# First batch's normalisations inside the second scan on ScalarE instead of VectorE, with softmax sums and gate remainders in PSUM

## What is computed

```python
# layer 0, mixer: normalise, project, convolve, then the selective scan
h = exp(dt_t * A) * h + (dt_t * x_t) * B_t ;  y_t = h @ C_t      # 256 steps, 256 x 16 states
y = (y + xc * D) * silu(z) ;  out = clamp(layernorm(clamp(y @ out_proj_w.T)))
x = x + out                                                        # skip
# layer 0, experts
t = layernorm(x) ;  xn = layernorm(t) * ln_g + ln_b
probs = softmax(xn @ gate_w) ;  combine = the two largest probs, 0 elsewhere
out = sum_e combine[:, e] * (gelu(xn @ w1[e] + b1[e]) @ w2[e] + b2[e])
t = x + layernorm(x) + out
# layer 1: x + decay scan over a row of channels, layernorm, 16 experts, top 2, no bias
```

## Time and profile before

| | us |
|---|---|
| median of 3 runs | 215.6 |
| lowest, highest | 214.52, 215.91 |
| profiled execution, its own time | 212.92 |
| its span in the trace | 211.0 |
| TensorE busy with matmuls | 180.6 |
| VectorE busy | 135.5 |
| ScalarE busy | 120.1 |
| GpSimd busy | 104.4 |

### The profile page before, as it was taken

One profiled execution on the slowest core, in us unless ns is written; L12 is line 12 of the kernel. 1 busy time (PEld: TensorE's weight loads), 2 busy tenths in 40 slices (PEclk: granted clock), 3 DMA queues, 4 the chain that ended last, 5 costly groups with the idle time before them and its releaser, 6 DMA issues. The chain is left out here.

```text
span 211.0 us, 3706 instructions
## 1 busy us (share of the span) xinstructions
PE 180.6 (86%) x1194; PEld 149.6 (71%) x1194; DVE 135.5 (64%) x317; ACT 120.1 (57%) x276; POOL 104.4 (49%) x136
## 2 busy tenths in 40 slices
PE   6789677995887387499999999699998999999993
PEld 5467454542353243267999989699997999999992
DVE  2764689999899999972373846563158573433433
ACT  2717995999850039143578646567564655455540
POOL 5410034579796955475575435444456244444500
PEclk9999999999999979999999999999999999999998
DMA  6950199995540000000000000000000000000000
GB/s 182 307 153 0 59 393 341 324 321 165 199 165 37 2 0 0 0 0 0 3 2 0 3 2 0 3 0 0 3 2 0 3 0 5 0 26 3 0 0 25
DMA packets 7233, 14.38 MB, mean 68 GB/s; under 512 B 512, under 2 KB 3112, under 8 KB 6960
## 3 DMA queue, kind: packets, MB, share of 16 engines
q1 hardware_dynamic: 7216, 14.17, 20.8%
HBM read 13.88 MB, written 0.29 MB: 67 GB/s over the span
## 5 line engine op out<-in xcount | busy, mean ns | idle before, releaser
L343 POOL TENSOR_TENSOR hc<-hs,cb 128x1024 f32<-128x1024 f32 x16 | 37.7, 2356 | 32.6 <-DVE hs L712 32.6
L836 DVE SCALAR_TENSOR_TENSOR acc<-dbx_ps,comb,acc 128x128 f32<-128x128 f32 x96 | 29.1, 344 | 36.6 <-PE dbx_ps L1106 35.6
L1081 PE MATMUL bc_ps<-x_hi,w_hi 128*128 128x256 f32 x128 | 41.8, 326 | 0.0
L563 ACT ACTIVATE hid<-bc_ps,par 128x256 f32<-128x256 f32 x64 | 26.8, 469 | 24.9 <-PE bc_ps L1083 24.8
L357 POOL TENSOR_TENSOR w_lo<-w1b,w_hi 128x256 fp32r<-128x256 f32 x32 | 23.5, 735 | 27.6 <-ACT w_hi L555 27.3
L712 DVE TENSOR_TENSOR_SCAN hs<-da,dbx_ps 128x1024 f32<-128x1024 f32 x16 | 36.5, 2278 | 0.1
L1083 PE MATMUL bc_ps<-x_hi,w_lo 128*128 128x256 f32 x128 | 36.2, 283 | 0.0
L1082 PE MATMUL bc_ps<-x_lo,w_hi 128*128 128x256 f32 x128 | 36.0, 281 | 0.0
L1106 PE MATMUL dbx_ps<-w2a,hid 128*128 128x128 f32 x256 | 34.1, 276 | 0.5 <-issue 0.3
L1106 PE MATMUL dbx_ps<-w2b,hid 128*128 128x128 f32 (+1 forms) x256 | 33.9, 276 | 0.5 <-DVE acc L836 0.5
L357 POOL TENSOR_TENSOR w_lo<-w1a,w_hi 128x256 fp32r<-128x256 f32 x32 | 23.1, 729 | 21.6 <-ACT w_hi L555 21.6
(11 more groups left out here) (164 smaller groups left out, 227.1 us busy)
## 6 DMA issues: line engine op xcount, KB each, us to landing
w1a<-w_in SPq DMA_DIRECT2D x2, 1024.0 KB, 9.0
cb<-c_rows SPq DMA_DIRECT2D x2, 1024.0 KB, 6.8
w1b<-w_in SPq DMA_DIRECT2D x2, 1024.0 KB, 13.7
cb<-c_rows SPq DMA_DIRECT2D x2, 768.0 KB, 5.2
cb<-taps_in SPq DMA_DIRECT2D x1, 512.0 KB, 5.2
cb<-c_rows SPq DMA_DIRECT2D x2, 256.0 KB, 3.8
par<-packed_in SPq DMA_DIRECT2D x1, 473.0 KB, 3.4
x_cm<-x_in SPq DMA_DIRECT2D x2, 128.0 KB, 2.2
```

The lines of the kernel that those rows point to most:

```text
L343: nc.gpsimd.tensor_tensor(hc[p][:], hs[p][:], cb[:, k].rearrange("p i (o t) -> p i o t", o=1).to_broadcast([128, PAIR, DC, T]), ALU.mult). ...
L563: ins = nc.scalar.activation(hid[p][:, c, :], h_ps[:, p, T * c:T * (c + 1)], ACT.Gelu, bias=par[:, bass.ds(u * UC + at, 1)])
L836: nc.vector.scalar_tensor_tensor(acc[k][:, t, :], o_ps[:, w // span % RING, 128 * t:128 * (t + 1)], comb[layer][b][:, t, bass.ds(u, 1)], a ...
L1081: nc.tensor.matmul(h_ps[:, p, T * c:T * (c + 1)], w1_hi[w][:, at], x_hi[b][:], start=True, stop=False)
```

## The change

Batch 0's normalisations of `skip_norm` and `inner_norm` are made by ScalarE as rstd * x + shift; GpSimd makes the new column `shift` = -mean * rstd after `root_3` and after `root_4`. `skip_scale` is a new step ahead of scan 2. ScalarE also scales `xg_tok` (`inner_scale`) and copies `combT` (`gates_tc`) for batch 0. VectorE keeps the clamp, the sums and the statistics, and all of batch 1. In every gating the remainder after the two largest (`left`) stands in PSUM instead of SBUF, and in `softmax_e` so does the reciprocal of the sum. In the diff `shifted` and the lines behind it are GpSimd's, `skip_scale` to the first `gates_tc` ScalarE's, and what follows from `skip_norm` VectorE's.

```diff
+        shift = sb("shift", [128, TT])
-        left = [[sb(f"left_{l}_{b}", [128, TT, EXPERTS[l] + 8]) for b in range(NB)] for l in range(2)]
+        m_zsum = m_ps[:, T + 32:T + 32 + TT]
+        m_left = [m_ps[:, T + 64:T + 64 + TT * (n + 8)].rearrange("p (t e) -> p t e", t=TT) for n in EXPERTS]
-        before_states = {1: ["gate_out", "out_proj"], 3: ["inner_norm", "root_5"], 4: ["logits"], 5: ["softmax_e"],
+        before_states = {1: ["gate_out", "out_proj"], 2: ["skip_scale"], 3: ["inner_norm", "root_5"], 4: ["logits"], 5: ["softmax_e"],
...
+            def shifted(k):
+
+                link(nc.gpsimd.tensor_tensor(shift[:], mv[0][:, :, 0], rstd[0][:], ALU.mult))
+                nc.gpsimd.tensor_scalar(shift[:], shift[:], -1.0, None, ALU.mult).then_inc(s["shift" + k], 1)
...
+                    if b == 0 and step in ("root_3", "root_4"):
+                        pool.wait_ge(s["rstd" + which], 1)
+                        shifted(which)
...
+            def skip_scale(layer, b):
+                act.wait_ge(s["shift3"], 1)
+                for t in range(TT):
+                    ins = nc.scalar.activation(m_norm[:, t, :], norm_a[b][:, t, :], ACT.Identity, scale=rstd[b][:, t:t + 1],
+                                               bias=shift[:, t:t + 1])
+                ins.then_inc(s["skip_scaled"], 1)
+
+            def inner_norm(layer, b):
+                if b:
+                    return
+                act.wait_ge(s["shift4"], 1)
+                for t in range(TT):
+                    ins = nc.scalar.activation(m_tok[:, t, :], t_tok[b][:, t, :], ACT.Identity, scale=rstd[b][:, t:t + 1],
+                                               bias=shift[:, t:t + 1])
+                ins.then_inc(s["inner_done"], 1)
+
+            def inner_scale(layer, b):
+                if layer or b:
+                    return
+                act.wait_ge(s["rstd5"], 1)
+                act.wait_ge(s["sum_done"], 1)
+                for t in range(TT):
+                    ins = nc.scalar.activation(xg_tok[b][:, t, :], m_tok[:, t, :], ACT.Identity, scale=rstd_b[b][:, t:t + 1])
+                ins.then_inc(s["xn_tok"], 1)
+
+            def gates_tc(layer, b):
+                if b:
+                    return
+                act.wait_ge(s["comb_ps"], b + 1)
+                nc.scalar.activation(combT[b][:], m_ps[0:EXPERTS[0], 0:T], ACT.Copy).then_inc(s["combT_ready"], 1)
...
             def skip_norm(layer, b):
                 dve.wait_ge(s["xtok_ready"], b + 1)
-                link(normalise(TT, m_norm, norm_a[b], mv[b], rstd[b], "rstd3", b))
+                if b:
+                    link(normalise(TT, m_norm, norm_a[b], mv[b], rstd[b], "rstd3", b))
+                else:
+                    dve.wait_ge(s["skip_scaled"], 1)
                 link(clamp(m_norm, m_norm))
...
             def inner_norm(layer, b):
-                link(normalise(TT, m_tok, t_tok[b], mv[b], rstd[b], "rstd4", b))
+                if b:
+                    link(normalise(TT, m_tok, t_tok[b], mv[b], rstd[b], "rstd4", b))
 
             def inner_scale(layer, b):
+                if (layer, b) == (0, 0):
+                    dve.wait_ge(s["inner_done"], 1)
+                    nc.vector.tensor_tensor(t_tok[b][:], t_tok[b][:], m_tok, ALU.add).then_inc(s["sum_done"], 1)
+                    return
...
-                link(nc.vector.reciprocal(zsum[b][:], zsum[b][:]))
+                link(nc.vector.reciprocal(m_zsum, zsum[b][:]))
                 link(nc.vector.tensor_tensor(prob[layer][b][:, :, 0:n], ex[:],
-                                             zsum[b][:].rearrange("p (t o) -> p t o", o=1).to_broadcast([128, TT, n]), ALU.mult))
+                                             m_zsum.rearrange("p (t o) -> p t o", o=1).to_broadcast([128, TT, n]), ALU.mult))
...
-                pr, rest_p = prob[layer][b], left[layer][b]
+                pr, rest_p = prob[layer][b], m_left[layer]
...
             def gates_tc(layer, b):
+                if b == 0:
+                    return
                 dve.wait_ge(s["comb_ps"], b + 1)
```

More of the change, by code:

```diff
@@ L85 @@
 b_ready dbx_done da_done h_done hc_done y_done
-yz_ready o_ps var3 rstd3 var4 rstd4 rstd5 xn_tok xn_ps x_full x_hi_ready xsplit logit_ps z_sub z_tanh comb_ready
+yz_ready o_ps var3 shift3 skip_scaled inner_done sum_done shift4 rstd3 var4 rstd4 rstd5 xn_tok xn_ps x_full x_hi_ready xsplit logit_ps z_sub z_tanh comb_ready
 comb_ps combT_ready b2_ps
@@ L528, in stage @@
                 high_part(0, u, u)
+            def skip_scale(layer, b):
[23 more added lines that the diff above has]
+                    return
+                act.wait_ge(s["comb_ps"], 1)
+                nc.scalar.activation(combT[b][:], m_ps[0:EXPERTS[0], 0:T], ACT.Copy).then_inc(s["combT_ready"], 1)
             def exp_logits(layer, b):
@@ L586, in _ @@
                     "bc_copy": bc_copy, "silu1": silu1, "stage": stage,
-                    "pair_in": pair_in, "exp_logits": exp_logits, "expert_in": expert_in,
+                    "pair_in": pair_in, "exp_logits": exp_logits, "skip_scale": skip_scale, "inner_norm": inner_norm, "inner_scale": inner_scale,
+                    "gates_tc": gates_tc, "expert_in": expert_in,
                     "softmax": softmax, "experts": experts}
```

## The result

The changed kernel takes 221.53 us (median of 4, 220.68 to 222.50) against 215.19 for the kernel before in the same comparison: ratio 1.0295, interval 1.023 to 1.036, 6.3 us more. Forecast were 3.3 more. Its four executions lie in two pairs (220.68 and 220.86, 222.19 and 222.50 us); the profiled one took 220.68 us, span 218.9.

A forecast was written before the change was run, and what follows sets the result against it. VectorE (97% busy) bounds the second scan; the start of TensorE's expert run at the first output matmul sets the end. Delay 0.97 inherited plus 2.56 new, less 0.23, gives +3.3 on 215.6: 218.9 us, range 217 to 221.

The forecast's parts named there:

- the queue's sum: Batch 1's scan to first output matmul: waits in ScalarE's ordered queue delay it 3.53 us; less 0.23 regained, +3.3 us.
- 94.96: Predicted time in us of TensorE's first output matmul in the changed kernel, instead of 91.43 before.
- VectorE's three waits: Signs in batch 1's scan: VectorE idle about 1.5 us before the t_tok sum, about 1.6 before scan 4, over 2 before scan 7.
- rival (d): ScalarE's switch to the Gelu table costs another 1.28 us beyond its load: 4.6 us in all, 220.2 us; chance 0.02.
- the term for TensorE's clock: At the first output matmul: the forecast sum added nothing for a lower TensorE clock behind the gap.
- rival (c): TensorE's clock halves for 3 us behind the gap before the first output: 1.5 us more, 4.8 in all, 220.4; chance 0.13.
- same pace of 1.6 us a unit: Sign of a right forecast: after the first output matmul, TensorE's expert work keeps 1.6 us a unit.
- the harmless one: TensorE's idle 2.79 us to 87.54 in the profile before, followed by 2.4 GHz pace; the predicted gap was 2.8 us.
- (a): Batch 1's scan: VectorE's relief wins, gates and first Gelu 2.6 us earlier, 213.0 us; chance 0.05.
- (b): Early hand-offs in batch 1's scan hidden, the last not: 0.3 us faster, 215.3 us; chance 0.10.
- the first two hand-offs: ScalarE's normalisations at pairs 2 and 3 of batch 1's scan: scan 4 1.53 us late, scan 5 0.97.
- the third: Hand-off at pair 6: gates' copy, decays of pair 7, table load and Gelu queue on ScalarE; 2.56 us new delay.

The follow-up runs named there:

- e3: The kernel before with one edit, batch 0's gates' copy to combT on ScalarE ahead of the decays of pair 7: 218.85 us, ratio 1.0191 to the kernel before.
- e4: The kernel before with the PSUM edits alone (reciprocal of the sum, remainder of the gates): 214.28 us, ratio 0.9959 to the kernel before.
- e1: The changed kernel with 12 identity matmuls in TensorE's idle stretch ahead of the first output matmul: 217.69 us, ratio 1.0149 to the kernel before.
- e6: The changed kernel again, unedited, for a second profile: 221.58 us, ratio 1.0277 to the kernel before.
- e9: e5 with the gates' copy on ScalarE as in the changed kernel: 215.05 us, ratio 0.9982 to the kernel before.
- e5: The changed kernel with w_hi and decays moved earlier in ScalarE's queue and the gates' copy back on VectorE: 214.34 us, ratio 0.9942 to the kernel before.
- e2: The changed kernel with batch 0's gates' copy to combT given back to VectorE: 216.56 us, ratio 1.0117 to the kernel before.
- e7: e5 with five identity matmuls behind each of the scan's sums of pairs 0 to 4 on TensorE: 213.37 us, ratio 0.9914 to the kernel before.

## Why the prediction came out as it did

**Right:** the direction, and the queue's sum. Scan 4: 1.53 us late worked out, 1.61 measured; scan 5: 0.97 and 1.06; first output: 3.53 and 3.63. With the start of this profile 1.57 us later, 94.96 would be 96.53, and the row stands at 96.63. Both products in PSUM: 0.17 each, as priced. ScalarE's pair with two columns: 0.84 for 0.83; with one: 0.62 for 0.70. VectorE's three waits: 1.71, 1.39 and 2.36 us for about 1.5, about 1.6 and over 2. The table load at 94.40 is followed by the Gelu at 95.69, so rival (d), a longer switch, is out.

**Wrong:** the term for TensorE's clock, which the sum put at nothing and left to rival (c) with a chance of 0.13 and a price of 1.5 us. The prediction's own sign of it, a granted clock under 1.0 after 95 us, came true; the "same pace of 1.6 us a unit" did not. "The gap is nearer to the harmless one. 0.13": the gap was 2.83 us, as said, and the clock fell behind it in both profiles of the changed kernel and in e3. The step that failed took two lengths of idle time (3.28 low, 2.79 not) for a threshold. They were one case each. Ahead of the sum of pair 5 the same gap is followed by a low clock in one profile and not in another: 2.24 us in e4 and e1 (2.25 in e6) but not in the changed kernel's first profile, 2.62 in e9 but not in e5. The price of 1.5 came from a single stretch of 3 us; two in a row are 6.8 us and 2.9. With (c) at its real price the sum is 3.3 + 2.9 = 6.2, where 6.3 was measured; the queue's part alone, 3.3, was 0.1 off the 3.4 of the profiles. At its own price of 1.5, (c) gave 220.4, still 1.1 short.

**The other rivals.** (a), VectorE's relief, does not occur in this order. What it would have needed, e5 gives, and it is worth 1.3 us by the medians and 1.43 at scan 5, not 2.6: the waits of 0.57, 0.32 and 0.27 us that e5's rows show take the rest. (b) fell with scan 4 at 21.02.

**The split of the 6.3 us:** 0.8 from the first two hand-offs net of 0.56 saved in prob's product (e2), 2.6 from the third by the queue (e3: 2.55; 1.6 decays, 0.95 copy with load and Gelu), 2.9 by the clock (after and e6 against the kernel before; 3.2 against e1). The comb8 product's 1.48 us brought nothing in the changed kernel, as worked out; where the Gelu is in time (e2, e4), it takes away no more than TensorE's wait of 0.23 us for hc of pair 6.

**Open:** which of TensorE's gaps lets the clock fall in a given execution. Ahead of the first output, idle times of 2.59, 2.82 and 2.83 us were followed by a low clock in three of three profiles, and those up to 1.94 us in none; but ahead of the sum of pair 5, 2.24 to 2.79 us were in four of ten. Profiles of one kernel differ there (after and e6), and a profiled execution and the median of its kernel by up to 2.3 us (212.92 and 215.19 for the kernel before).

## What to carry to other kernels

Relief for the busiest engine is worth what the receiving engine's queue leaves of it: list what stands behind each new waiting instruction, and put everything that is ready ahead of it. If the new wait opens a gap on TensorE ahead of its densest work, price the clock as likely and not as an accident (here it fell in all three profiles with such a gap), at half speed over the longest low stretch that any profile shows. A single case on either side is no threshold. Filling the gap with idle matmuls, or closing it by order, takes that part away.

## What the hardware showed unexpectedly

- The stretches of low clock were 3.4 us long (e4, e9, and e3 behind the first output) or 6.8 (the changed kernel behind the first output, twice), and came not always right behind the idle time: in e3 it began 2.1 us into the work.
- One place was steady: ahead of the spread that stands at 72.91 in the kernel before, TensorE idles 3.2 to 3.3 us, and a low clock followed, or had just begun, in all ten profiles that have this idle time. In e7, where 2.09 us of it are left, none did.
- Where the stretch falls decides what it costs. The changed kernel's profile has two in the scan (75.7 to 79.2 and 82.5 to 86.0 us) and e1's only the first of them, yet scans 4 and 5 stand within 0.02 us of each other; the one behind the first output cost 2.9 us.
- The idle time just ahead does not decide it: 2.24 us were followed by a low clock in e4 (3.58 us for four matmuls) and not in the changed kernel (1.98).
- A product of 128x16 with a second input in SBUF can cost 1.65 us beside GpSimd and costs 0.17 with that input in PSUM.
